# Attention weighting split by key rows: each half of the weighting matmuls issued beside the other pass

## The reference, cut to what matters

```
q, k, v: (4, 16 heads, 2048, 16)      q = q * 16**-0.5
scores = einsum('bqhd,bkhd->bhqk', q, k)
probs  = softmax(scores, axis=-1)
out    = einsum('bhqk,bkhd->bqhd', probs, v)
```

## Time and profile before

| | |
|---|---|
| median of 3 runs | 3724.8 us (3721.16 to 3727.24) |
| the profiled execution | 3726.17 us, its span 3724.5 us |
| mean granted TensorE clock | 0.953 |
| PE, PEld, DVE, ACT, POOL busy | 92%, 45%, 82%, 67%, 12% of the span |
| `attend` | from about 770 to 3640 us of the span |
| one head in mid-kernel, turn to turn | 42.7 us |

### The profile page before, as it was taken

How to read it: one execution, slowest core, us unless ns; L and a number is a source line. 1 busy time by engine, 2 the same in 40 slices (tenths; PEclk the granted TensorE clock), 3 DMA queues, 4 the chain that set the end, 5 groups by cost and what they waited for, 6 DMA issues and landing times. The chain is left out here.

```text
span 3724.5 us, 67174 instructions
## 1 busy us (share of the span) xinstructions
PE 3441.4 (92%) x19888; PEld 1679.6 (45%) x19888; DVE 3050.0 (82%) x3113; ACT 2480.1 (67%) x4784; POOL 451.7 (12%) x470
## 2 busy tenths in 40 slices
PE   7848888779999999999999999999999999999997
PEld 6427777634443434434434434434434444344435
DVE  7886777678887888888878888888878888888844
ACT  3544333327777777777767777777777777777772
POOL 3534555500000000000000000000000000000004
PEclk9978999959998999999989999999999999999999
DMA  3662222111111111111111111111111111111115
GB/s 105 196 180 69 56 62 56 50 40 41 41 45 38 49 45 44 45 43 41 41 41 41 46 41 49 45 41 43 41 41 41 46 41 49 45 39 45 42 31 193
DMA packets 101398, 213.01 MB, mean 57 GB/s; under 512 B 11392, under 2 KB 59584, under 8 KB 88832
## 3 DMA queue, kind: packets, MB, share of 16 engines
q1 hardware_dynamic: 90320, 199.29, 17.8%
q10 hardware_dynamic: 10800, 10.01, 0.9%
HBM read 148.42 MB, written 59.77 MB: 56 GB/s over the span
## 5 line engine op out<-in xcount | busy, mean ns | idle before, releaser
L1161 DVE TENSOR_REDUCE half_max<-m_ps 128x1 f32<-128x1024 f32 x2048 | 2414.5, 1219 | 417.5 <-PE m_ps L1079 409.3
L1026 ACT ACTIVATE prob<-s_ps 128x512 f32<-128x512 f32 x4096 | 2130.7, 603 | 659.1 <-PE s_ps L1095 646.7
L1095 PE MATMUL s_ps<-q_feat,k_feat 50*128 50x512 f32 x4096 | 1522.9, 453 | 43.3 <-issue 29.4
L1079 PE MATMUL m_ps<-k_feat,q_feat 48*128 48x512 f32 x4096 | 1385.5, 454 | 38.9 <-DMA k_feat<-k_parts 28.6
L1095 PEld LDWEIGHTS s_ps<-q_feat,k_feat 50*128 50x128 f32 x4096 | 694.1, 188 | 1283.3 <-ACT prob L1026 1109.0
L1104 PE MATMUL a_ps<-prob,v_head 128*32 128x512 f32 x8192 | 1117.2, 618 | 31.3 <-issue 31.3
L1079 PEld LDWEIGHTS m_ps<-k_feat,q_feat 48*128 48x128 f32 x4096 | 639.6, 192 | 141.0 <-DVE half_max L1161 61.0
L1104 PEld LDWEIGHTS a_ps<-prob,v_head 128*32 128x32 f32 x8192 | 164.9, 109 | 285.9 <-issue 193.3
L931 POOL TENSOR_TENSOR shift<-row_max,shift 128x16 fp32r<-128x16 f32 x64 | 14.1, 221 | 1996.2 <-ACT shift L1031 1996.2
L704 ACT ACTIVATE g_hi<-g 128x512 fp32r<-128x512 f32 x128 | 80.9, 632 | 252.0 <-DVE g L736 247.8
L820 POOL TENSOR_TENSOR g_lo<-g,g_hi 128x512 fp32r<-128x512 f32 x128 | 183.5, 1434 | 222.7 <-ACT g_hi L704 222.7
(11 more groups left out here) (144 smaller groups left out, 1789.3 us busy)
## 6 DMA issues: line engine op xcount, KB each, us to landing
q_feat<-q_parts SPq DMA_DIRECT2D x128, 256.0 KB
k_feat<-k_parts SPq DMA_DIRECT2D x128, 256.0 KB
q_parts<-parts SPq DMA_DIRECT2D x32, 512.0 KB, 4.8
k_parts<-parts SPq DMA_DIRECT2D x32, 512.0 KB, 4.7
mask_bc<-mask_b SPq DMA_DIRECT2D x128, 128.0 KB, 3.3
q_feat<-q_parts SPq DMA_DIRECT2D x128, 128.0 KB
k_feat<-k_parts SPq DMA_DIRECT2D x128, 128.0 KB
att_dram<-att SPq DMA_DIRECT2D x64, 256.0 KB, 15.9
```

Of the source, the lines that this page charges most:

```text
L1026: act.activation(prob[tile(r, kt) % R][:, qb * BLK:(qb + 1) * BLK], s_ps[slot(r, kt, qb, turn) % R][:, :], ACT.Exp).then_inc(exped, 1)
L1079: ins = pe.matmul(m_ps[p % 2][:, k * BLK:(k + 1) * BLK], q_feat[r % 2][LOW, qt * P:(qt + 1) * P], k_feat[r % 2][LOW, key:key + BLK], start ...
L1095: pe.matmul(s_ps[slot(r, kt, qb, turn) % R][:, :], k_feat[r % 2][UP, kt * P:(kt + 1) * P], q_feat[r % 2][UP, qb * BLK:(qb + 1) * BLK], sta ...
L1161: dve.tensor_reduce(half_max[r][:, p // 2, p % 2:p % 2 + 1], m_ps[p % 2][:, :], AX.X, ALU.max).then_inc(maxed, 1)
```

## The change

The weighting of a key tile is cut in two by key rows. `weigh_low` multiplies keys 0 to 63 of the tile (array rows 0 to 63), `weigh_up` keys 64 to 127 (rows 64 to 127). Both accumulate in `a_ps`, so 8 matmuls of 64 rows stand where 4 of 128 rows stood. A new semaphore `weighed_low` makes `weigh_up` wait until `weigh_low` of the same tile has ended, and `weigh_low` waits on `weighed` until `weigh_up` of the tile before has ended. In the order of a step `weigh_low` moves to the front, ahead of the first score matmul; the second matmul of pair `a` moves behind the second score matmul; `weigh_up` stands ahead of pair `b`; the third score matmul moves behind pair `b`. ScalarE's, VectorE's, GpSimd's and SyncE's orders are as before.

```diff
-            def weigh(g, r, kt, turn):
+            def weigh_low(g, r, kt, turn):
                 if kt == 0:
                     pe.wait_ge(v_ready, g + 1)
                     pe.wait_ge(att_read, g + 1)
                 pe.wait_ge(exped, slot(g, kt, QB - 1, turn) + 1 + R)
+                wait_apart(pe, weighed, tile(g, kt) + R, t["passed"][1])
                 for qb in range(QB):
-                    ins = pe.matmul(a_ps[qb * VW:(qb + 1) * VW, :], v_head[r % R][:, kt, :],
-                                    prob[tile(r, kt) % R][:, qb * BLK:(qb + 1) * BLK],
-                                    start=(kt == 0), stop=(kt == ST - 1))
+                    ins = pe.matmul(a_ps[qb * VW:(qb + 1) * VW, :], v_head[r % R][0:UPPER, kt, :],
+                                    prob[tile(r, kt) % R][0:UPPER, qb * BLK:(qb + 1) * BLK], start=(kt == 0), stop=False)
+                ins.then_inc(weighed_low, 1)
+
+            def weigh_up(g, r, kt):
+                wait_apart(pe, weighed_low, tile(g, kt) + 1, t["passed"][1])
+                for qb in range(QB):
+                    ins = pe.matmul(a_ps[qb * VW:(qb + 1) * VW, :], v_head[r % R][UPPER:P, kt, :],
+                                    prob[tile(r, kt) % R][UPPER:P, qb * BLK:(qb + 1) * BLK], start=False, stop=(kt == ST - 1))
                 ins.then_inc(weighed, 1)
...
+                    if weighs:
+                        weigh_low(*late)
                     score(g, it, r, kt, 0, following)
                     a(0)
-                    a(1)
                     score(g, it, r, kt, 1, following)
                     if following and kt == TURN_AT:
                         turn(g + 1, turn_slot(g), turn_slot(r) % R)
-                    if kt >= LAG:
-                        weigh(g, r, kt - LAG, following)
-                    elif not first:
-                        weigh(g - 1, r - 1, ST + kt - LAG, True)
-                    score(g, it, r, kt, 2, following)
+                    a(1)
+                    if weighs:
+                        weigh_up(*late[:3])
                     b(0)
                     b(1)
+                    score(g, it, r, kt, 2, following)
                     score(g, it, r, kt, 3, following)
```

More of the change, by code:

```diff
@@ L885, in attend @@
     exped = sem("a_exped")
-    weighed = sem("a_weighed")
+    weighed, weighed_low = sem("a_weighed"), sem("a_weighed_low")
     v_ready = sem("a_v_ready")
@@ L1119, in step @@
                     a, b = half(kt, 0), half(kt, 1)
+                    if kt >= LAG:
+                        late = (g, r, kt - LAG, following)
+                    else:
+                        late = (g - 1, r - 1, ST + kt - LAG, True)
+                    weighs = kt >= LAG or not first
+                    if weighs:
+                        weigh_low(*late)
                     score(g, it, r, kt, 0, following)
                     a(0)
-                    a(1)
                     score(g, it, r, kt, 1, following)
@@ L1149, in _ @@
             for kt in range(ST - LAG, ST):
-                weigh(HEADS - 1, HEADS - 1, kt, False)
+                weigh_low(HEADS - 1, HEADS - 1, kt, False)
+                weigh_up(HEADS - 1, HEADS - 1, kt)
         @block.vector
```

## The result

The changed kernel takes 7283.3 us (7281.6 to 7286.0, four runs), the kernel before on the same chip 3726.0: a ratio of 1.953, 95% interval 1.946 to 1.960. Forecast were 3519 us, with a range of 3440 to 3740.

What follows compares the result with a forecast made beforehand. No engine was always busy; a 2.60 us chain of exponent, scores and weighting bound each step. Per head -14 x 0.30 + 0 + 0.96 = -3.24, times 64 = -207 against 3726.2: 3519 us, range 3440 to 3740.

Steps and rivals of the forecast that it cites:

- So the rows seem to decide, not the columns.: TensorE weighting: 64x32 tiles may run beside 64x128 tiles in the other row half, giving a step of 2.30 us.
- The row on columns: Profile timeline where 64-column tiles on all rows change to 128-column tiles without waiting; next matmul follows 0.22 later.
- the drain rival: TensorE drains at every change of shape, so nothing runs beside a block: about 4880 us, chance 0.17.
- By that rule 3.73.: Attention step in us if changing tiling mode drains TensorE, with score 2 behind both matmuls of pair b.
- The clock drops: the head ran at 1.00, and the array gets denser, 0.01.: Rival on TensorE's granted clock: it falls below the 1.00 at which the head ran; chance 0.01.
- Step 2.30 in 14 steps: Ordinary attention steps fall from 2.60 to 2.30 us, -0.30 in each of 14 a head.
- VectorE late next: Ordinary steps: after TensorE, VectorE's reductions come next as bound, 2.28 us a step if never idle.
- Step kt = 2, +0.96: Step waiting for ScalarE's copy of `a_ps`: 4.13 us instead of 3.17, since more matmuls stand behind that wait.
- Turn about 0: Turn step of a head: keeps both shape changes and stays at 3.06 us, change about 0.
- Dispatch, ScalarE's wait, transfers: nothing: Other costs: 16 more TensorE instructions a step, two self-waits, ScalarE's wait for `weighed` and unchanged transfers add nothing.

Runs made afterwards that it cites:

- bare stretches 7 and 8: Kernel of bare matmuls: four 32-column matmuls on lower rows, 128-column ones on upper rows; mixed data types, then all float32; 1.66 and 2.05 us a round.
- 4, 5 and 9: Same bare kernel, equal widths in both row halves: 4 x 32 columns, 128 columns, 128 float32 beside 2 x 128; 0.86, 0.23 and 0.87 us a round.
- 10 to 12: Same bare kernel: 64 beside 128 columns in row halves; full rows, 64 and 128 columns; full rows, 4 x 32 and 128; 2.53, 2.06, 2.05 us a round.
- The run with full blocks: Changed kernel with all 128 rows in both weighting blocks, same order, waits and instruction count: 4639.4 us.
- the clock was lifted by force: Changed kernel with bursts of 24 dense full matmuls put in: 7246.9 us with one burst a loop round, 6305.8 us with one in each head.
- the order alone: Kernel before with its whole 128-row weighting block at the front of the step, other matmuls in the changed kernel's order: 3866.0 us, ratio 1.038.
- the old order: Kernel before with its weighting block split into two 64-row blocks at the old place, with the changed kernel's waits: 7293.0 us; with a burst once a round 7417.0 us.
- the wide halves: Changed kernel with each weighting half as two matmuls of 128 columns in place of four of 32: 9068.4 us.

## Why the prediction was wrong, step by step

- **"So the rows seem to decide, not the columns."** This step failed, and with it the whole gain. No block of 64x32 tiles runs beside 64x128 tiles: bare stretches 7 and 8 (1.66 and 2.05 us a round, one behind the other) against 4, 5 and 9 (0.86, 0.23 and 0.87) show it. The row on columns was a case of its own, transposes, and I built on it without a pair of plain matmuls. The rule that I quoted from the Trainium skill (TensorEngine Tiling (Array Packing), Key Properties: another mode drains) was right for plain matmuls, as stretches 7, 8 and 10 to 12 bear out, and so was the drain rival in kind. At 0.17 it was rated far too low.
- **"By that rule 3.73."** Measured 3.31 at 2.4 GHz. I had score 2 stand behind both matmuls of pair b. In the trace it starts beside the first of them (3000.94 and 3000.95), ahead of the second, as scores 0 and 1 do with pair a: 0.34 + 0.32 behind each block instead of 0.76 and 0.99. The run with full blocks, which is the rival's case with the clock up, took 4639 us where the rival said 4880.
- **"The clock drops: the head ran at 1.00, and the array gets denser, 0.01."** The clock was a term put at nothing, and this was the largest error: 2644 of the 3557 us. I looked at how full TensorE's time was and not at how much of the array a block addresses. Nothing overlaps, so the array gets emptier, each block on 64 rows, and the 1.2 GHz of the lead-in is never left (and where the clock was lifted by force, it went again at the stall that the new order adds). Neither my range nor any rival holds 7283.
- **Step 2.30 in 14 steps; VectorE late next.** Not reached: VectorE stands idle over half of the time.
- **Step kt = 2, +0.96.** With the order alone: 4.18 against 3.17, +1.01. Right, but I had not priced the lapse of the clock behind such a stall, 81 us in that kernel. With two full blocks the step takes 5.33, 2.01 over an ordinary one; forecast were 1.83 over.
- **Turn about 0.** 3.09 against 3.06 with the order alone: right there. With two full blocks, where nothing overlaps, it takes 3.96, +0.90.
- **Dispatch, ScalarE's wait, transfers: nothing.** Two full blocks have the same instructions, semaphores and transfers as the changed kernel and a step of 3.32, all of it accounted for by blocks and scores: right. The waits of TensorE for its own counts show when the halves touch: 0.18 a step in the old order.

## What to carry to other kernels

Before you count on matmuls running beside each other in different array rows, find a pair of exactly those tile widths in a trace, or run the pair by itself; rows of transposes are no evidence. Put the granted clock in every forecast as a term of its own: a change that leaves fewer array rows addressed can double the time of TensorE while its busy share stays at 95%, so ask from what clock a stage starts and what would lift it. And where a loop's branch stops TensorE, count what the clock loses behind the stop, not only the stop.

## What the runs showed that I had not expected

- 64, 72 and 104 rows in one kind of matmul out of three left the whole of attention at 0.50, 120 rows gave 0.96, and zeros in half of the values changed nothing (0.98).
- A dense stream on the lower 64 rows stayed at 1.2 GHz for 85.5 us when begun there and kept 2.4 GHz for its 34.5 us, all that was tried, when begun at that; both halves together rose to 0.94 and 0.96 (mean of the stretch).
- A stall of 1.95 us was enough to lose 2.4 GHz behind weighting on 64 rows, and there it did not return for the rest of the round; behind the same stall the kernel with two blocks of 128 rows kept it or was back within 3 to 10 us.
- A change of tile width alone, on the same rows, costs 0.17 us between plain float32 matmuls; a transposed tile of 64 columns ahead of one of 128 costs nothing.
- TensorE's instructions start out of their program order across row halves: score 2 before the second matmul of pair b, 3000.95 and 3001.53.
- The end of a loop round costs 8 to 9 us, a fifth of a head: a stop of about 3 us, and the rest behind it.

**Open.** What happens with counts of rows between 104 and 120, why 120 rows are at 1.2 GHz for longer than 128, and what exactly loses 2.4 GHz in the old order and in bare stretch 10 without a stall. Whether a halved weighting of equal width and rounded type could pay was not tried: the wide halves tried here stream twice as much.
